# Order of the condition's DMA and of the last query chunk's eviction in a graph-attention kernel

## The reference

```python
q_exp = where(x.sum(-1) == 0, 0, cond)
self_feat = concat(x, q_exp) @ W_self.T + b_self
output = self_feat
for d in range(2):                       # two directions of the edges
    A = adj or its transpose, first 20 neighbours
    mask, bias = A.sum(-1) > 0, A @ w_bias + b_bias
    qh = self_feat @ Wq[d].T + bq[d]     # 16 heads of 32
    kh = self_feat[:, :20] @ Wk[d].T + bk[d]
    w = softmax(where(mask, qh.kh / sqrt(32), NEG) + bias)
    output += (w @ self_feat[:, :20]) @ Wout[d] + bout[d]
return x + relu(output)
```

## Time and profile before

| | |
|---|---|
| median of three runs | 2041.55 us |
| profiled execution | 2035.38 us, span 2033.6 us |
| TensorE matmul | 1934.0 us, 95% |
| VectorE | 1338.7 us, 66% |
| GpSimd | 841.0 us, 41% |
| ScalarE | 568.0 us, 28% |
| DMA | 220.89 MB, mean 109 GB/s |

### The profile page before, as it was taken

The page is one execution under the profiler, slowest core; times in us unless marked ns, Lnnn a source line. Parts: engine busy times, 40 slices in busy tenths (PEclk is TensorE's granted clock), DMA queues, the critical chain, the costliest instruction groups (busy, mean ns, idle before and its releaser), DMA issues.

```text
span 2033.6 us, 34072 instructions
## 1 busy us (share of the span) xinstructions
PE 1934.0 (95%) x10888; PEld 1679.7 (83%) x10888; DVE 1338.7 (66%) x1898; ACT 568.0 (28%) x1150; POOL 841.0 (41%) x723
## 2 busy tenths in 40 slices
PE   5899999999999999999999999999999999999999
PEld 3899999978778888788888788888887888888887
DVE  6623223277677777777777777777777777777776
ACT  2232231332222222222222222222222222222221
POOL 1413122154444444444444444444444444444443
PEclk9999999999999999999999999999999999999999
DMA  9423322364434444444444444444444344444431
GB/s 171 78 84 76 95 70 67 98 153 122 110 104 116 116 115 115 113 110 116 109 115 110 114 110 116 115 116 114 110 116 113 108 107 116 108 115 116 116 105 64
DMA packets 240765, 220.89 MB, mean 109 GB/s; under 512 B 57808, under 2 KB 195536, under 8 KB 236624
## 3 DMA queue, kind: packets, MB, share of 16 engines
q1 hardware_dynamic: 236256, 220.28, 42.6%
q10 hardware_dynamic: 4464, 0.02, 0.1%
HBM read 165.44 MB, written 54.79 MB: 108 GB/s over the span
## 4 chain that ended last, share of the span: by engine, by line
PE 43%; SPq 14%; DMA 10%; issue 7%; DVE 5%; ACT 1%; ACTq 0%; POOL 0%; DVEq 0%
PE bank L1306 26%; SPq L887 10%; DMA res<-c_dram 9%; PE bank L1254 7%; PE bank L1278 6%; PE bank L1267 2%; DVE res L1050 2%; SPq L840 2%; PE bank L1242 2%; DVE res L1052 2%; DVE sm L1040 1%; ACT sc L1144 1%; SPq L837 1%; SPq L833 1%; SPq L862 1%
## 5 line engine op out<-in xcount | busy, mean ns | idle before, releaser
L940 POOL TENSOR_TENSOR rc<-nzb,cqg 128x512 f32<-128x512 bf16 x256 | 265.1, 1041 | 409.0 <-DVE qt_main L1065 409.0
L1242 PEld LDWEIGHTS bank<-kbd,qt_main 128*128 128x128 f32 x2048 | 243.6, 192 | 33.2 <-issue 25.6
L1242 PE MATMUL bank<-kbd,qt_main 128*128 128x80 f32 x2048 | 247.2, 274 | 14.0 <-DVE qt_main L1065 14.0
L1040 DVE TENSOR_REDUCE sm<-sc 128x32 f32<-128x640 f32 x128 | 104.6, 817 | 235.4 <-ACT sc L1144 235.4
L918 POOL TENSOR_TENSOR sc<-sc,mx 128x640 f32<-128x640 f32 x128 | 163.4, 1276 | 227.1 <-DVE mx L1034 227.1
L1065 DVE SCALAR_TENSOR_TENSOR qt_main<-bank,bq_all,rc 128x512 f32<-128x512 f32 x256 | 186.9, 730 | 83.4 <-PE bank L1306 75.9
L928 POOL TENSOR_TENSOR wt<-sc,rs 128x640 f32<-128x640 f32 x128 | 163.1, 1274 | 135.2 <-DVE rs L1043 133.6
L1152 ACT ACTIVATE wtt<-bank 128x384 f32<-128x384 f32 (+1 forms) x256 | 111.1, 435 | 378.0 <-PE bank L1267 377.9
L1306 PE MATMUL bank<-nodes_h,wq_h 128*128 128x512 f32 x512 | 210.1, 410 | 2.6 <-DVE qt_main L1065 2.6
L1306 PE MATMUL bank<-xh_odd,wq_h 128*128 128x512 f32 x512 | 210.4, 411 | 0.0
L1306 PE MATMUL bank<-xh_odd,wq_l 128*128 128x512 f32 x512 | 202.0, 395 | 0.0
(11 more groups left out here) (120 smaller groups left out, 3947.9 us busy)
## 6 DMA issues: line engine op xcount, KB each, us to landing
rows<-in_x SPq DMA_DIRECT2D x128, 256.0 KB, 5.0
xk<-in_x SPq DMA_DIRECT2D x32, 1024.0 KB, 6.0
res<-c_dram SPq DMA_DIRECT2D x32, 1024.0 KB, 6.7
out<-res SPq DMA_DIRECT2D x128, 256.0 KB, 2.1
adj<-in_mask_BxSxSx_ik SPq DMA_DIRECT2D x32, 440.0 KB, 3.8
adj<-in_mask_BxSxSx_ik SPq DMA_DIRECT2D x128, 110.0 KB
k_dram<-kv_kst SPq DMA_DIRECT2D x64, 160.0 KB, 1.8
v_dram<-kv_vt SPq DMA_DIRECT2D x256, 40.0 KB
```

The source lines that it names most:

```text
L940: pool.tensor_tensor(rc[:, c % 2, :].rearrange("p (b n) -> p b n", b=G), nzb[:, par, :].rearrange("p (b n) -> p b n", b=G), cqg[:, par, c, ...
L1040: nc.vector.tensor_reduce(sm[:, b % 2, :], sc[:, b % 2, :].rearrange("p (h m) -> p h m", m=NG), AX.X, ALU.add).then_inc(sum_ready, 1)
L1242: mm = nc.tensor.matmul(dst, qt[:, c, b * N:b * N + N], kbd[:, c, :, b * NG:b * NG + NG], start=True, stop=True)
```

## The change

The condition's DMA is issued ahead of the wait for `m_done` and of the five DMAs of the edges. On VectorE the eviction of the last query chunk goes ahead of the third transpose of x, where it stood behind it.

```diff
@@ -886,11 +886,11 @@
                 for c, s, lo, hi in value_pieces():
                     sp.dma_start(vbd[lo - P * c:hi - P * c, c, s, :],
                                  vv[lo:hi].rearrange("r b e -> r (b e)")).then_inc(vbd_loaded, 16)
+                load_condition(g)
                 if not last:
 
                     sp.wait_ge(m_done, 2 * g + 2)
                     load_edges(g + 1)
-                load_condition(g)
                 store(g, 0)
                 if last:
                     for b in range(1, G):
@@ -1094,9 +1094,9 @@
                 q_evacuate(6)
                 if not last:
                     turn(g + 1, 1 - par, 1)
+                q_evacuate(7)
+                if not last:
                     turn(g + 1, 1 - par, 2)
-                q_evacuate(7)
-                if not last:
                     turn(g + 1, 1 - par, 3)
                 if first:
                     nonzero_rows(0, 0)
```

More of the change, by code:

```diff
@@ L1096, in group @@
                     turn(g + 1, 1 - par, 1)
-                    turn(g + 1, 1 - par, 2)
                 q_evacuate(7)
                 if not last:
+                    turn(g + 1, 1 - par, 2)
                     turn(g + 1, 1 - par, 3)
```

## The result

The changed kernel takes 1953.59 us (median of four runs, 1952.21 to 1954.26) against 2042.31 us before; the ratio is 0.957, with an interval of 0.955 to 0.959. The profiled execution took 1954.26 us, its span is 1952.5 us. The forecast was 1953 us.

A forecast was written before the change was run, and what follows sets the result against it. TensorE, busy 95%, was taken to bound the kernel with its idle waits and clock dips. Terms 55.9 + 13.7 + 15.9 = 85.5 us took 2035.4 to 1950, carried to 1953 us; range 1938 to 1980 us.

The forecast's parts named there:

- The clock's share: TensorE at `self_features(3)`: nine groups at 1.2 GHz behind the stall return to full clock, 13.7 us (bounds 0 and 13.7).
- The stall ahead of `self_features(3)`: TensorE's wait for VectorE to take batch 0's bank, put down to the condition's late landing, goes whole: 55.9 us.
- the value of the last group: Condition's DMA: without edges just ahead, the transfer takes 4.6 us as in the last group, not 6.99 us.
- The term of zero for the edges: Edges issued 0.5 us later, behind the condition; first read over 14 us after their issue, so priced at zero.
- The rule on transposes from the Trainium skill: Three transposes ahead of `self_features(3)` do not count as busy for the clock; some dips might stay, up to 13.7 us less gain.
- The eviction: VectorE's eviction of chunk 7 ahead of the third transpose: `scores(0)` 0.70 us earlier, net 0.53 us a group, 15.9 us in all.
- the 0.10 us by which the first matmuls of a waiting `scores` are longer: `scores(0)`, no longer waiting, runs 1.91 us instead of 2.01; counted within its 0.70 us in each of 30 groups.
- The margin of 0.6 us at `self_features(3)`: After the change, VectorE's release of batch 0's bank comes 0.6 us before TensorE could start `self_features(3)`.
- the 3 us that I carried to the median: Half of the 6.2 us between earlier median and profiled execution, part perhaps extra clock dips; raised 1950 to 1953 us.
- No effect: Rival: the condition is not what holds ScalarE's exponential, so its earlier issue gains nothing; 2041 us, chance 0.06.
- the shrunken stall: Rival: the stall at `self_features(3)` keeps 0.5 us in 28 groups and the dips stay; 1980 us, chance 0.17.
- The slower one: Rival: VectorE waits for chunk 7 ahead of two transposes, delaying `m1` and `scores(1)`, with added dips; 2052 us, chance 0.04.

The follow-up runs named there:

- the first part alone: Against the changed kernel, the eviction of chunk 7 stays behind two transposes, with only the condition moved ahead of the edges; 1967.25 us, ratio to before 0.964.
- the edges' experiment: Against the changed kernel, edges issued ahead of the values' 20 pieces, the condition behind both, so issued as late as before the change; 1960.34 us.
- The second part alone: Against the changed kernel, the condition stays behind the edges, with only the eviction of chunk 7 ahead of the third transpose; 2053.86 us, ratio 1.0067.

## Why the prediction was right

The time was right (1953 forecast, 1953.59 measured), and each of the two parts was run by itself. The clock's share was not: the dips went together with the stall.

**The stall ahead of `self_features(3)` goes whole, 55.9 us, and the dips with it, 13.7 us.** Together 69.6 us; the first part alone gave 71 us (2038.31 to 1967.25). The landing took the value of the last group, 4.6 us, give or take 0.4 us, in every group, and the edges' experiment shows that this comes from what is ahead in the queue. The term of zero for the edges held too: they land later (5.6 us instead of 3.8), but VectorE waits for them once in the whole span, for 0.9 us. The rule on transposes from the Trainium skill that the prediction weighed ("TensorE: Matmul & The Clock Gate", section "Part 4: PE-mode transpose") did not show: the three transposes are still there, and from 415 us to TensorE's last matmul at 1948 us the granted clock of the changed kernel is 1.00. One reading was of a single group: in the nine groups with a dip the first matmul took 0.50 to 0.80 us, and 0.50 us behind a stall without a dip, so it is the length of the 12 matmuls (about 4.6 us against 3.06) that tells the two apart.

**The eviction, 0.53 us a group, 15.9 us.** Measured behind the first part: 13.7 to 14.2 us, 0.46 to 0.47 us a group. The new limit was the one named, `m1`, and the eviction waits for nothing. What was mis-sized is the 0.10 us by which the first matmuls of a waiting `scores` are longer. I took it off `scores(0)` and did not put it on `scores(1)`, where it now is. With it the stall there is 0.14 + 0.10 = 0.24 us, and the copy of `m1` ahead of the last high part got that back.

**What is late next.** The margin of 0.6 us at `self_features(3)` held, with 0.63 us in the group shown: the kernel with the late issue and the short transfer starts to stall, by little, in some groups. With the landing still earlier nothing more came.

**The sum against the profiled execution.** Forecast 85.5 us, measured 2035.38 - 1954.26 = 81.1 us. From the first `self_features` of the main loop (433.40 us before, 435.75 after) to the end of the span it is 1600.2 - 1516.7 = 83.5 us; the other 2.4 us lie ahead of that, where the change can hardly act yet: the first instruction that it moves, the condition's DMA, is issued at 434.25 us. There the changed kernel's profiled execution has a mean granted clock of 0.57 from 407 to 415 us, where the one before has 1.00. Five of the eight traces have such a dip there, and what decides it is open. The missing 2.0 us in the loop are covered by the 0.10 us in 30 groups, 3 us. That the time was met to 0.6 us is in part luck: the profiled execution was forecast 4.4 us too low (1950 against 1954.26 us), and the 3 us that I carried to the median made up for it, though the changed kernel's median lies below its profiled execution and not above. So the gain by medians (88.7 us) is larger than by profiles. That the slower runs of before had more dips was argued, and no trace of them shows it. The granted clocks speak for it in part: of the twelve executions of the kernel before, the three slowest (2045 to 2047 us) have 0.981 to 0.984 and the nine others (2036 to 2039 us) 0.985 to 0.988, but in the set of seven two executions of 2039 and 2040 us have 0.983 and 0.984 as well. The second part alone, with 19 dips, scatters most (2049 to 2063 us), while the kernels without dips in the main loop stay within 2.1 us.

**The rivals.** No effect and the shrunken stall are out by the waits. The slower one did not occur, but its two mechanisms are real: a wait of VectorE ahead of the transposes costs its full length in each group, and a longer stall at `self_features(3)` brings more dips. What failed in it is the assumption that a stall ahead of `scores(1)` would also lower the clock each time: of 31 such stalls of 0.95 to 1.0 us none did. The stall of 1.37 us that the rival had in mind was not made, so this is shown for the shorter one alone.

## What to carry to other kernels

The gains from two stalls in one loop of TensorE need not add up. Ask of each whether its end is pinned by something that doesn't move when TensorE comes earlier: such a stall swallows every gain ahead of it, and must be removed first. A transfer that gates an engine belongs ahead of bulky ones with time to spare in the same queue, and here that pays twice, by its issue time and by its length. When an instruction is moved ahead of a wait, look for work of just the length of that wait to leave in front of it.

## What the runs showed of the hardware

- A load of 1024 KB took 4.5 to 4.9 us (medians of six kernels) with no edges issued just ahead of it, and 6.7 to 6.8 us (medians of two) behind 880 KB of edges: about 2 us more. Issued 0.6 us ahead of the same edges it took 4.6 us, and the first 440 KB of these 5.6 us instead of 3.8.
- The lower level of TensorE's clock (1.2 GHz) came behind some stalls and not behind others: in the main loop 9 times with 28 stalls of 1.3 to 3.0 us of idle time, 19 times with 28 stalls of 1.9 to 3.1 us, never with 31 stalls of about 1.0 us. A stall of 3.04 us kept full clock in one group, so the idle time alone does not decide it.
